# Attention scores on 64x128 tiles of the array, outputs on 128x64 tiles over the whole contraction

## The reference

```python
lat = layer_norm(layernorm(x), lat_g, lat_b)          # 64 x 256
ctx = layer_norm(context, ctx_g, ctx_b)               # 1024 x 256
q = (lat @ Wq)      # 16 heads of 64 columns: 64 x 64 per head
k, v = split(ctx @ Wkv)                               # 1024 x 64 per head, each
k = apply_rope(k, cos, sin)
attn = softmax(clip(q @ k.T * 64 ** -0.5, -11, 11))   # 64 x 1024 per head
out = attn @ v                                        # 64 x 64 per head
x = x + concat_heads(out) @ Wo + bo
```

## Time and profile before

| | |
|---|---|
| Median of 3 runs | 1230.54 us (1227.43 to 1234.68) |
| The profiled execution | 1237.52 us, its span 1235.8 us |
| TensorE busy | 1183.8 us, 96% of the span |
| VectorE / ScalarE / GpSimd busy | 1021.3 / 650.5 / 609.2 us |
| Mean granted TensorE clock | 0.989 of full speed |

### The profile page before, as it was taken

The page is one execution under the profiler, slowest core; times in us unless marked ns, Lnnn a source line. Parts: engine busy times, 40 slices in busy tenths (PEclk is TensorE's granted clock), DMA queues, the critical chain, the costliest instruction groups (busy, mean ns, idle before and its releaser), DMA issues.

```text
span 1235.8 us, 39825 instructions
## 1 busy us (share of the span) xinstructions
PE 1183.8 (96%) x16268; PEld 998.4 (81%) x16268; DVE 1021.3 (83%) x1954; ACT 650.5 (53%) x1089; POOL 609.2 (49%) x611
## 2 busy tenths in 40 slices
PE   7999999999999999999999999999999999899997
PEld 3778788878778788778877878778888788789997
DVE  6799889989888899889988988889767366668886
ACT  7556555554545555545554545555444233356674
POOL 2466556555655555556555655556443133333332
PEclk8999999999999999999999999999999999999999
DMA  6366565556555566555656656565653530566662
GB/s 231 80 165 155 147 149 137 143 139 170 144 135 150 138 154 158 142 134 134 151 143 153 149 134 147 138 148 142 167 114 100 188 127 31 190 205 174 204 197 64
DMA packets 136173, 181.36 MB, mean 147 GB/s; under 512 B 30316, under 2 KB 96312, under 8 KB 135864
## 3 DMA queue, kind: packets, MB, share of 16 engines
q1 hardware_dynamic: 110552, 150.80, 45.8%
q10 hardware_dynamic: 21360, 23.80, 7.6%
q0 software_dynamic: 4080, 4.22, 1.7%
HBM read 81.93 MB, written 30.56 MB: 91 GB/s over the span
## 4 chain that ended last, share of the span: by engine, by line
PE 87%; DVE 4%; issue 3%; DMA 2%; ACT 2%; SPq 1%; POOL 1%; POOLq 0%; ACTq 0%; DVEq 0%
PE bank L1579 29%; PE bank L1608 27%; PE bank L1565 10%; PE bank L1934 6%; PE bank L1631 3%; PE bank L1738 2%; PE bank L1984 2%; PE bank L1985 2%; PE bank L1986 1%; PE bank L1791 1%; PE bank L1815 1%; PE bank L1834 1%; DMA x_slots<-xn_all,slot 1%; DMA w_two<-in_L_ffn_W_dram 1%; PE bank L1824 1%
## 5 line engine op out<-in xcount | busy, mean ns | idle before, releaser
L1579 PE MATMUL bank<-ct,wk_hi 128*128 128x512 f32 x1024 | 328.6, 402 | 5.3 <-DVE kr_third L1119 3.1
L1608 PE MATMUL bank<-p_hi,xc 128*128 128x512 f32 x1024 | 316.1, 390 | 0.0
L1579 PEld LDWEIGHTS bank<-ct,wk_hi 128*128 128x128 f32 x1024 | 189.7, 190 | 46.3 <-DVE kr_third L1119 3.7
L1118 DVE TENSOR_TENSOR kw<-bank,stab 128x512 f32<-128x512 f32 x256 | 175.7, 686 | 62.0 <-PE bank L1579 56.1
L1608 PEld LDWEIGHTS bank<-p_hi,xc 128*128 128x128 f32 x1024 | 192.1, 188 | 39.9
L593 POOL TENSOR_TENSOR kr<-kr,ksw 128x1024 f32<-128x1024 f32 x64 | 154.4, 2412 | 106.8 <-issue 104.0
L1579 PE MATMUL bank<-ct,wk_lo 128*128 128x512 f32 x512 | 202.2, 395 | 0.0
L1608 PE MATMUL bank<-p_lo,xc 128*128 128x512 f32 x512 | 199.3, 389 | 0.0
L783 ACT CAST p_hi<-pr 128x1024 fp32r<-128x1024 f32 x128 | 134.4, 1050 | 95.2 <-DVE pr L1086 95.2
L1106 DVE TENSOR_TENSOR p_lo<-pr,p_hi 128x1024 fp32r<-128x1024 f32 x128 | 169.0, 1321 | 0.5 <-ACT p_hi L783 0.4
L778 ACT ACTIVATE pr<-bank 128x1024 f32<-128x1024 f32 x128 | 126.8, 1026 | 61.1 <-PE bank L1565 61.1
(11 more groups left out here) (227 smaller groups left out, 2023.5 us busy)
## 6 DMA issues: line engine op xcount, KB each, us to landing
ksw<-kw SPq DMA_DIRECT2D x512, 128.0 KB, 2.3
x_turned<-xt SPq DMA_DIRECT2D x120, 128.0 KB
ct_read<-x_turned SPq DMA_DIRECT2D x30, 512.0 KB
w_two<-in_L_ffn_W_dram SPq DMA_DIRECT2D x15, 1024.0 KB, 5.0
raw<-in_ctx_dram ACTq DMA_DIRECT2D x56, 256.0 KB, 3.9
x_slots<-fill ACTq DMA_DIRECT2D x32, 258.0 KB, 3.7
w_all<-in_L_ffn_W_dram SPq DMA_DIRECT2D x4, 2048.0 KB, 17.2
wo<-in_L_ffn_W_dram SPq DMA_DIRECT2D x7, 1024.0 KB, 5.2
```

The source lines that it names most:

```text
L1118: dve.tensor_tensor(by_tile(kw[:, i, cols]), keys_, by_tile(stab[:, places]), ALU.mult).then_inc(kw_done, 1)
L1579: last = pe.matmul(psK[:, a * 512:(a + 1) * 512], l[:, k, w], ct[:, h % 3, r, k], start=(m == 0), stop=(m == len(parts) - 1))
L1608: last = pe.matmul(psZ[c], xc[:, slot_, l, t, cols], r[:, i, :, t], start=(f == 0 and m == 0), stop=(f == 1 and m == len(parts) - 1), skip ...
```

## The change

Scores: the loop over the halves of 64 keys (`c`) is gone. One matmul takes 64 rows and all 128 keys of a block as weights, and writes 128 partitions. A step has 16 program matmuls in place of 32, on two row tiles (`h`) in place of four tiles.

Outputs: the loop over the halves of the contraction (`r`) is gone. One matmul contracts over 128 rows, with weights of 128 rows and 64 columns, on two column tiles (`h`). A quad has 16 program matmuls in place of 32, and the result stands in one bank (1, or 3 for the last two quads) in place of two.

VectorE: `added` and its 32 calls are gone; `divided` waits for ScalarE's copy, which now holds the whole sum. `o_sum` counts one event a quad (the reciprocals), and TensorE's waits on it become waits on `o_half`; the one ahead of the keys moves to the second pair of the step, the one whose keys go to bank 1.

```diff
-        def out_bank(n, r):
-            return bank[:, r, 0:4 * N] if n < QUADS - 2 else (bank[:, 5, D:D + 4 * N], bank[:, 3, 0:4 * N])[r]
+        def out_bank(n):
+            return bank[:, 1 if n < QUADS - 2 else 3, 0:4 * N]
...
-                    sp.wait_ge(o_sum, 2 * n + 1)
+                    sp.wait_ge(o_sum, n + 1)
...
-                    act.copy(o_part[:], out_bank(n, 1)).then_inc(o_half, 1)
+                    act.copy(o_part[:], out_bank(n)).then_inc(o_half, 1)
...
-            def added(n):
-                dve.wait_ge(o_half, n + 1)
-                dve.tensor_tensor(o_part[:], out_bank(n, 0), o_part[:], ALU.add).then_inc(o_sum, 1)
...
-                dve.wait_ge(o_sum, 2 * n + 2)
+                dve.wait_ge(o_half, n + 1)
...
-                            for c in range(2):
-                                cols = slice(a * 512 + t * P + c * N, a * 512 + t * P + (c + 1) * N)
-                                for h in range(2):
-                                    rows = slice(h * DH, (h + 1) * DH)
-                                    last = pe.matmul(banks[c * N:(c + 1) * N, h, t * 2 + a], kr_at(j)[rows, cols], qo[rows, g, at:at + N],
-                                                     start=True, stop=True)
+                            cols = slice(a * 512 + t * P, a * 512 + (t + 1) * P)
+                            for h in range(2):
+                                rows = slice(h * DH, (h + 1) * DH)
+                                last = pe.matmul(banks[:, h, t * 2 + a], kr_at(j)[rows, cols], qo[rows, g, at:at + N], start=True, stop=True)
...
+                        if a == 1 and due(j, 12):
+                            pe.wait_ge(o_half, (j - 12) // 4 + 1)
...
-                wait(pe, o_sum, 2 * n)
+                wait(pe, o_half, n)
...
-                        for r in range(2):
-                            rows = slice(r * DH, (r + 1) * DH)
-                            for h in range(2):
-                                last = pe.matmul(out_bank(n, r)[h * DH:(h + 1) * DH, i * N:(i + 1) * N], wv[rows, k, g * P + h * DH:g * P + (h + 1) * DH],
-                                                 zt[rows, k, (i // 2 * 4 + h * 2 + i % 2) * N:(i // 2 * 4 + h * 2 + i % 2 + 1) * N], start=(k == 0), stop=(k == KC - 1))
+                        for h in range(2):
+                            last = pe.matmul(out_bank(n)[h * DH:(h + 1) * DH, i * N:(i + 1) * N], wv[:, k, g * P + h * DH:g * P + (h + 1) * DH],
+                                             zt[:, k, (i // 2 * 4 + h * 2 + i % 2) * N:(i // 2 * 4 + h * 2 + i % 2 + 1) * N], start=(k == 0), stop=(k == KC - 1))
...
-                if due(j, 8):
-                    pe.wait_ge(o_sum, (j - 8) // 2 + 2)
```

More of the change, by code:

```diff
@@ L1131, in two_steps @@
                 blocks_turned(j - 1)
-                if due(j, 8):
-                    added((j - 8) // 4)
                 shifts(j)
@@ L1343, in _ @@
             projected(0)
-            added(QUADS - 2)
             normalise(0, 0)
@@ L1348, in _ @@
             projected(1)
-            added(QUADS - 1)
             divided(QUADS - 1)
@@ L1754, in _ @@
             scores(STEPS - 3)
-            pe.wait_ge(o_sum, 2 * QUADS - 4)
+            pe.wait_ge(o_half, QUADS - 2)
             pe.wait_ge(vec2_ld, 32)
@@ L1775, in _ @@
             sums(STEPS - 2)
-            pe.wait_ge(o_sum, 2 * QUADS - 2)
+            pe.wait_ge(o_half, QUADS - 1)
             turn(0)
```

## The result

The kernel after takes 1310.74 us (median of 4 runs, 1310.49 to 1310.90) against 1230.93 us before (4 runs, 1227.43 to 1234.68): a ratio of 1.0648, 95% interval 1.0616 to 1.0679. It is 80 us slower, within the range and 6 us under the forecast of 1317. The runs after lie within 0.4 us of each other, those before within 7.

The account below looks back on a forecast made before the run. TensorE was taken as the bound, busy 1183.8 of 1235.8 us. On the profiled 1237.5 us, +112.6 for scores, +4 for seams and -34 for stalls gave 1320; allowing for the median, 1317 us, range 1301 to 1350.

Parts of the forecast that it names:

- What sets the pace of the scores: TensorE's scores: weight load by columns, a round 58 to 60 ns for 64 columns, 111 to 117 for 128.
- Scores: TensorE's score steps: 57.2 ns a record, a pair 3.66 us against 1.90, +1.76 us; 64 pairs, +112.6 us.
- Outputs: TensorE's outputs: 0.93 us against 0.95, no gain or loss; a new seam of 0.13 in 32 quads, +4 us.
- The addition: VectorE's L1094, 0.39 us 32 times: its 12.5 us lie beside the path, so removing it frees nothing.
- Stalls: TensorE in the steady part: 34 us lost to late instructions, taken as gone with fewer instructions, -34 us.
- the rest: Part of the 34 us lost in stalls beyond the idle time put down to issue, ascribed to reduced clock.
- The median: Whole kernel: profiled execution 7 us above the median; 1313 if the excess stays, 1320 if stalls; taken 1317.
- The step that failed: Under the scores: TensorE has no idle time beside them that could hide their +112.6 us.
- The rival of the records: Scores and outputs: number of records sets the pace, 14.9 ns each; 1131 us; 0.06 with the 29 ns rival.
- the one of 29 ns: A record costs 29 ns on any split under four 64x64 tiles; 1207 us; 0.06 with the records rival.
- The rival of loads that don't overlap: Scores: row tiles of 64 don't overlap loads, 111.5 ns a record; 1540 us; 0.02 with anything else.
- The rival of stalls that stay: TensorE's stalls stay, nothing given back: 1354 us, or 1347 by the median; 0.14 in whole or good part.

Follow-up runs that it names:

- the three experiments on it: Against the kernel after: heads one behind the other, 1689.83 us; half of the queries streamed, 1343.09; queries as weights and keys streamed, 1201.62.
- one row tile at a time: Kernel after with the loop over the two heads outside, so 32 records in turn use the same row tile: 1689.83 us.
- the swapped roles: Kernel after with a head's 64 queries as weights and 128 keys streamed, on four 64x64 tiles in turn: 1201.62 us, 0.9739.
- the scores moved apart: Kernel before, but in steps that hold outputs the second scores run behind the keys and the sums: 1298.79 us, 1.0523.
- half of the queries: Kernel after, but from the third step on only 32 of a head's 64 queries are streamed past the same weights: 1343.09 us.
- two other runs: Kernel before with only the outputs on 128x64 tiles and no addition, 1217.59 us; kernel before with second scores behind keys and sums, 1298.79 us.
- the runs that thinned the stream: Against the kernel before: outputs' new shape alone, 1217.59 us; that with outputs two steps earlier between keys and sums, 1212.19; second scores moved, 1298.79.

## Why the prediction was right

Point by point, by its own steps.

- **What sets the pace of the scores** was right, and is shown by the three experiments on it. Weights of 64 and 128 columns are one to two in time; the tiles of different rows share a load; the number of records doesn't count, and the streamed columns don't while they are no more than those of the weights.
- **Scores**, +1.76 us a pair of steps: measured 3.72 - 1.97 = 1.75 and 3.72 - 2.03 = 1.69. The pace forecast was 57.2 ns, from L1815. Start to start, a round of two takes 112 ns, 56 a record, the lower bound from L1934. L1815's later rounds of four take 112 ns as well: the forecast's length of the group also holds the 0.2 us between its first round and its second. Over 64 pairs the term is 110 us in place of 113.
- **Outputs**, no change but a seam of 0.13: measured +0.10 us a quad, 3 us in place of 4.
- **The addition**, nothing: shown by putting it back. The waits on `o_half` are never felt, as argued.
- **Stalls**, -34 us: measured, since 29 quads took 823.1 us before and 1005.09 - 113.24 = 891.9 after, while 29 times (30.75 - 27.20) would be +103. The difference is 34 us, the whole of it. Of the 34 us, 24.5 are idle time. The granted clock fell behind three of the 16 stalls only, the longest (2.15, 2.07 and 2.03 us); the quads with them lost 1.9 us each on top of the idle time, 5.8 in all. So the clock is less than the forecast's "the rest"; the other 4 us are mostly 0.1 to 0.4 in each of the other quads with a stall, and their cause is open.
- **The median.** I set 1317 between two readings of the 7 us by which the profiled execution stood above the median: 1313 if the excess stays, 1320 if it was stalls. After the change, where no stall is left, the profiled execution (1310.49) and the median (1310.74) agree, which speaks for the second reading; the runs without a profile have no trace to show it. By that reading the sum was 9 to 10 us too high. Held against the spans below, 5.5 of it lie ahead of the steady part (7.0 forecast, 1.6 found; the next point), 2.8 in its 29 quads (scores and seam together) and 1.3 behind.
- **The step that failed** is a sentence under the scores: "TensorE has no idle time beside it that could hide this". Ahead of the steady part it had some. Before, TensorE waited at 88.5 us for VectorE's product of the keys, once:

```profile
PE bank L1579 <- DVE kr_third L1119: 2.7, 1, 2.7
```

That is the line of the waits from 50 to 112 us before. The stretches of the sums ahead of it (with the wait) and of the keys behind it, before (length, busy times, granted clock, DMA share, GB/s):

```profile
85.70:91.23 5.53, 2.88 (x13) 2.07 (x12) 5.50 (x9) 1.22 (x2) 2.71 (x3) 1.00 0.21 82
91.23:95.69 4.46, 4.46 (x13) 3.53 (x13) 4.43 (x9) 4.37 (x7) 1.94 (x2) 0.62 0.58 133
```

After the change each of the two takes 2.72 us at full clock: 4.5 us lost before, and given back. Four pairs of scores lie ahead of the first outputs, worth 6.7 us, and the first scores start 0.6 us earlier (53.94 for 54.55). So the first outputs start only 1.6 us later than before.

The spans add up: 68.7 us more in the steady part (891.85 - 823.11), 1.6 ahead of it (113.24 - 111.66), and 2.6 behind ((1308.7 - 1005.09) - (1235.8 - 934.77)), where two pairs stand: together 72.9, as 1308.7 - 1235.8. The medians differ by 80, as the profiled execution of before stood 7 us above its median.

The rival of the records and the one of 29 ns are refuted by L1556's 57 ns beside the 29 ns of the swapped roles. The rival of loads that don't overlap is refuted, too: it is what happens on one row tile at a time. The rival of stalls that stay did not come true.

On the rule of the Trainium skill (TensorEngine Tiling (Array Packing), Instruction Overhead) that was weighed against the rows, not to cut a dimension that is already small for the sake of tiling: the change stopped cutting the keys for the sake of tiling, and lost 1.7 us a pair. The 14.9 ns a record of the 64x64 tiles before lie below a cost by the matmul of 60 cycles, 25 ns at 2.4 GHz (an estimate from the figure of the Trainium skill); the 29 ns of the swapped roles don't decide it.

## What to carry to other kernels

When the streamed operand has no more columns than the weights, a group of matmuls costs its weight loads: count columns of weights, divided by the tiles that load side by side, not instructions. When it has more, the stream takes the place of the load (109 ns a round for 128 streamed columns past 64). Tiles side by side help only if they are used in turn. Splitting 128 weight columns in two column tiles doubles the records and halves the time, and making the operand with fewer columns the weights halves the records at the same time. Where small tiles make the instruction stream dense, keep dense groups apart: fewer instructions in the outputs gave 1.3% here and moving them 0.4% more, and look for what then becomes late (the scores moved apart lost 5%).

## What the runs showed of the hardware that I had not expected

- **The granted clock falls while TensorE is busy without a break.** With one row tile at a time it was 0.71 to 0.91 in the scores of the steady part and 0.50 to 0.60 in the keys behind them. With two row tiles and 32 streamed columns it fell in 11 of 29 quads, to 0.50 to 0.67 in keys. With 64 streamed columns it stayed at 1.00 over 900 us. The profile counts TensorE as busy in all three. It cost about 32 us in the quads with half of the queries, and about 210 us (an estimate, above) with one row tile at a time. What exactly makes it fall was not tried.
- **A stall can cost more than its idle time.** After 2.15 us of idle time, 12 key matmuls took 4.45 us for 2.86. This followed the three longest of the 16 stalls before, and none of the others. The runs with stalls also vary more: 7 us between the fastest and slowest before, 0.4 after; that the stalls are the reason was not tried.
- **In the stalls TensorE goes on only 1.2 to 1.6 us after an instruction packet has ended**, on top of the 0.9 to 1.8 us that the packet itself takes. So 2.2 to 3.2 us pass from the start of the packet, more than the 1.9 us that 256 instructions (128 records of 14.9 ns) last at the pace of the 64x64 tiles. That the wait is for this packet is inferred from 16 coincidences before, 14 in two other runs, and from the runs that thinned the stream. The stalls that stayed in the kernel with the scores apart, and the one in a pair of steps without outputs, show that the number of 256 instructions in a run is no sharp bound.
